# A four-layer kernel: the sequential stages of a batch rebuilt as a slotted pipeline over batches, scores through DRAM

## The chip, the core and the metric

The kernel runs on one core of a Trainium2 chip. The metric is the device time of one execution in microseconds, lower is better. A core has a matrix engine (TensorE; PE in the rows, PEld its weight loads), VectorE (DVE), ScalarE (ACT), GpSimd (POOL), and SyncE (SP), which here issues all DMA. Each engine runs its own queue of instructions strictly in order and meets the others only at semaphores.

## What is computed

The input is eight batches of 512 tokens with 128 features. Four residual layers follow one another, each closed by a layer norm without weights:

```
x = norm(x + attn0(x))    # 16 heads of 8, rotary, causal softmax
x = norm(x + ffn0(x))     # silu(x W1) * (x W2), then gelu(. H1), gelu(. H2), W3; hidden 512
x = norm(x + attn1(x))    # 16 heads of 64, 4 memory keys, l2-normed q and k:
                          #   dots = W_pre @ (10 q.k)   (heads mixed), causal
                          #   keep the 64 largest of each row, softmax, W_post @ attn
                          #   out = (attn @ v) * head_scale * sigmoid(x Wg + bg), then Wo
x = norm(x + moe(x))      # 16 experts of 64, top 4 of the softmaxed gates, and a shared expert
```

Batches don't depend on each other.

## The kernel before

**Stages.** `network` opens with `start` (first batch only), then a hardware loop over eight batches, whose body is `front`, a conditional `again`, and `experts`. Each is a block: five queues, one per engine, that all begin and end together, with the semaphores cleared behind it. `again` (a full selection of the 64 largest) runs only if a flag says that the quick search missed.

**`front`** does for batch b, in turn: attention 0 (transposed scores, L1182, exponentials on ACT at L1309 and L1312, products with values at L1196), the feed-forward layer (L1238, L1240, L1248, with Silu and Gelu at L1317 to L1321), keys and queries of attention 1 (L1269, L1272, squares and norms on DVE and POOL), then `scores_*`.

**`scores_*`** is the second attention. The 512 query rows are cut into 64 pieces of 8 rows (`R8`), each 8 rows x 16 heads = 128 partitions, and taken in pairs: 32 steps, with a pipeline behind each. A step's score rows are up to 516 wide (`width`), and the query tiles come in the order 3, 1, 0, 2 (`TILE_ORDER`). For one pair:
- PE makes q.k for two heads at a time (L614); ACT and, for the first tile, DVE scale and store it to `dots` in SBUF (L772, L989);
- SP loads eight rows of all heads from `dots` to `mixin`, SBUF to SBUF (L553);
- PE mixes heads (L666) and ACT copies the result to `xs` (L790);
- DVE takes the row maximum and moments (L857, L859), POOL a first threshold (L580 to L583), then three rounds: ACT counts what lies above it (L799), POOL corrects it (L589 to L591);
- ACT exponentiates (L810), DVE finds the exact 64th value near the threshold (L912 to L929) and masks (L952), POOL scales the post-mix weights by the row sum (L567, L574), PE mixes heads again, transposed (L679), ACT stores it (L821);
- once in four steps PE multiplies with the values (L705, L710), DVE gates (L963), and once in eight PE applies Wo (L719) and DVE adds the residual (L969).

The step loops of the engines (`for s in range(...)` in `scores_tensor`, `scores_scalar`, `scores_vector`, `scores_gpsimd`) write out by hand what of step s, s-1, s-2, s-3 and s-4 stands where. PSUM has four rings of two banks: a (PE to ACT), o (PE to DVE), m (head mix) and t (post mix). A matmul into a ring waits until the bank before last has been read.

**`experts`** does the fourth layer of batch b and beside it the rotary projections of batch b+1 (L1034 to L1046), their split into three bf16 parts on POOL (L1024 to L1028), their way through DRAM into the stacked layout (L1011, L1017), and the row maxima of attention 0 for the first eight heads (PE L1066 and L1070, DVE L1084). The other eight heads' maxima stand in `front`. The experts' products are L1463 (Silu on ACT, L1498), L1465 and L1468 (products on DVE, L1536 and L1540) and L1478.

## Time and profile before

| | us |
|---|---|
| median of 3 runs | 4687.48 |
| lowest and highest | 4676.58, 4687.7 |
| the profiled execution | 4677.0 |
| its span, first to last instruction | 4675.4 |
| busy: PE, DVE, ACT, POOL | 3245.3, 2600.1, 2074.2, 1379.7 |

The program is eight nearly identical batches. One of them, from 3531 to 4106 us of the span, is read here: `front` up to the first head mix (3531 to 3712), the second attention (3712 to 4015), `experts` (4015 to 4106). The steps of the second attention are timed by the DVE instruction L861, one for each pair.

### The profile page before, as it was taken

The numbers are of one execution on the slowest core, as the hardware profiler recorded it, in microseconds if no ns is written. First come the engines' busy times: TensorE is split into PE (matmuls) and PEld (weight loads), VectorE is DVE, ScalarE is ACT, GpSimd is POOL, SyncE is SP. The second block draws the span as 40 slices with busy tenths as digits, with TensorE's granted clock in tenths as the row PEclk, the third lists the DMA queues.
The fourth block names the chain that finished last, engine by engine and source line by source line (L and its number), as shares of the span: only waits on it lengthen the run. The fifth ranks groups of instructions, "written<-read, shape, count | busy, mean of one in ns | idle before, by whom it ended". The sixth has DMA issues, their size and how long they took to land. (4 is left out here: it accounts for less than half of the span.)

```text
span 4675.4 us, 63627 instructions
## 1 busy us (share of the span) xinstructions
PE 3245.3 (69%) x19124; PEld 1917.1 (41%) x19124; DVE 2600.1 (56%) x9042; ACT 2074.2 (44%) x5898; POOL 1379.7 (30%) x3919
## 2 busy tenths in 40 slices
PE   3777567675786757767667776687766777667766
PEld 1345423453334532345323453235532355323543
DVE  2367743666436664466643775437753477534774
ACT  1356413664226642266322763227622376124770
POOL 1035501354013540145301453014520145102551
PEclk6877778777687777977778777787787877778787
DMA  2021210212102120022200221002210112101111
GB/s 89 1 37 24 47 47 0 40 27 52 36 0 41 29 53 32 0 43 30 51 29 7 40 33 46 29 15 33 32 45 29 20 29 31 45 29 28 23 30 48
DMA packets 99769, 151.99 MB, mean 33 GB/s; under 512 B 19518, under 2 KB 86998, under 8 KB 96126
## 3 DMA queue, kind: packets, MB, share of 16 engines
q1 hardware_dynamic: 99326, 146.87, 15.4%
q8 instruction: 182, 2.98, 0.3%
q14 instruction: 261, 2.14, 0.1%
HBM read 64.90 MB, written 9.59 MB: 16 GB/s over the span
## 5 line engine op out<-in xcount | busy, mean ns | idle before, releaser
L666 PE MATMUL pm<-mixin,pre_b 128*128 128x258 f32 (+15 forms) x1088 | 466.7, 552 | 343.0 <-ACT xs L790 160.6
L505 POOL TENSOR_TENSOR rstd<-var,powers 128x4 f32<-128x4 f32 x32 | 32.5, 1015 | 1623.3 <-DVE var L515 1623.3
L679 PE MATMUL pt<-wsc,attn 128*128 128x128 f32 x2560 | 445.2, 333 | 87.0 <-POOL wsc L574 86.3
L614 PE MATMUL pa<-kT,qT 64*128 64x132 f32 (+3 forms) x1024 | 327.2, 533 | 239.8 <-ACT dots L772 128.7
L679 PEld LDWEIGHTS pt<-wsc,attn 128*128 128x128 f32 x2560 | 391.6, 236 | 168.5 <-POOL wsc L574 123.7
L799 ACT ACTIVATE ex<-xs,thr 128x420 f32<-128x420 f32 (+12 forms) x624 | 347.6, 560 | 179.2 <-POOL thr L591 149.6
L666 PEld LDWEIGHTS pm<-mixin,pre_b 128*128 128x128 f32 x1088 | 216.4, 244 | 478.4 <-issue 321.7
L1084 DVE TENSOR_REDUCE dots<-po 128x1 f32<-128x384 f32 (+3 forms) x374 | 222.9, 638 | 339.8 <-PE po L1070 339.8
L857 DVE MAX8 top<-xs 128x8 f32<-128x420 f32 (+15 forms) x384 | 163.5, 434 | 441.3 <-ACT xs L790 440.4
L589 POOL TENSOR_SCALAR shift<-signs 128x2 f32<-128x2 f32 x624 | 127.6, 205 | 677.7 <-ACT ex L799 340.7
L772 ACT ACTIVATE dots<-pa,rq 128x388 f32<-128x388 f32 (+3 forms) x512 | 228.0, 473 | 208.9 <-PE pa L614 169.9
L614 PEld LDWEIGHTS pa<-kT,qT 64*128 64x128 f32 x1024 | 168.2, 234 | 333.2 <-ACT dots L772 177.4
L705 PE MATMUL po<-at,vx 128*64 128x64 f32 x5120 | 241.0, 259 | 63.4 <-ACT at L821 59.4
L705 PEld LDWEIGHTS po<-at,vx 128*64 128x64 f32 x5120 | 222.2, 170 | 86.3 <-ACT at L821 71.2
L821 ACT COPY at<-pt 128x384 f32<-128x384 f32 (+3 forms) x512 | 196.1, 426 | 131.4 <-PE pt L679 130.8
L580 POOL TENSOR_TENSOR spreads<-meanvar,powers 128x2 f32<-128x2 f32 x208 | 157.1, 755 | 302.1 <-DVE meanvar L865 302.1
L574 POOL TENSOR_SCALAR wsc<-post_b,rsum 128x128 f32<-128x128 f32 x512 | 218.5, 437 | 26.2
L799 ACT ACTIVATE squares<-tokens,thr 128x452 f32<-128x452 f32 (+6 forms) x336 | 186.8, 559 | 88.0 <-POOL thr L591 64.8
L567 POOL TENSOR_TENSOR rsum<-ssum,powers 128x2 f32<-128x2 f32 x256 | 181.6, 709 | 113.7 <-DVE attn L952 96.4
L921 DVE MAX8 best<-left 128x8 f32<-128x420 f32 (+12 forms) x416 | 203.1, 488 | 0.0
L921 DVE MAX8 best<-squares 128x8 f32<-128x420 f32 (+12 forms) x416 | 198.9, 478 | 0.0
L799 ACT ACTIVATE squares<-xs,thr 128x420 f32<-128x420 f32 (+5 forms) x288 | 160.7, 562 | 74.2 <-POOL thr L591 60.8
(261 smaller groups left out, 7613.7 us busy)
## 6 DMA issues: line engine op xcount, KB each, us to landing
dots<-moe_dram SPq DMA_DIRECT2D x8, 2176.0 KB, 9.2
kT<-parts_dram SPq DMA_DIRECT2D x216, 64.0 KB
dots<-ffn_dram SPq DMA_DIRECT2D x8, 1536.0 KB, 6.8
at<-ffn_dram SPq DMA_DIRECT2D x8, 1280.0 KB, 10.7
mixin<-dots SPq DMA_DIRECT2D x32, 258.0 KB
mixin<-dots SPq DMA_DIRECT2D x32, 242.0 KB
mixin<-dots SPq DMA_DIRECT2D x32, 226.0 KB
parts_dram<-at SPq DMA_DIRECT2D x18, 384.0 KB, 4.0
```

Source lines behind the costliest of these rows:

```text
L567: chain.link(nc.gpsimd.tensor_tensor(rsum[:, p], ssum[:, p], powers[:, TT + PAIR:], ALU.pow))
L574: nc.gpsimd.tensor_scalar(wsc[:, m % A_SLOTS], post_b[:, :], rsum[:, p, z:z + 1], 1.0, ALU.mult, ALU.mult).then_inc(attn_done, 1)
L614: nc.tensor.matmul(bank_of(("qk", t, 2 * c + odd, z))[:, 0:jn], qT_v[at:at + HD1, c, P * t:P * t + P], kT_v[at:at + HD1, c, j0:j0 + jn], s ...
L666: ins = nc.tensor.matmul(bank[:, 0:jn], pre_b[:, :], mixin[:, m % MIX_SLOTS, j0:j0 + jn], start=True, stop=not last)
L679: ins = nc.tensor.matmul(bank[:, P * k:P * k + P], attn[:, m % A_SLOTS, P * k:P * k + P], wsc[:, m % A_SLOTS], start=True, stop=True)
L705: ins = nc.tensor.matmul(bank[at:at + HD1, col:col + RB], vx_v[:, k, HD1 * h:HD1 * h + HD1], at_v[:, k, h, :], start=k == 0, stop=k == t a ...
L772: nc.scalar.activation(dots[:, at:at + jn], banks_a[A.bank(key)][:, 0:jn], ACT.Copy, scale=rq[:, t, g:g + 1]).then_inc(a_free, 1)
L799: ins = nc.scalar.activation(ex[m % E1_SLOTS][:, 0:width(n)], xs[m % X_SLOTS][:, 0:width(n)], ACT.Sign, scale=-1.0, bias=thr[:, s % LIVE, ...
L821: nc.scalar.copy(at_v[:, 0:t + 1, :, R8 * u:R8 * u + R8], bank[:, 0:P * (t + 1)].rearrange("p (k h i) -> p k h i", k=t + 1, h=H1)).then_in ...
L857: found = chain.mark(nc.vector.max(out=top[:, p, z], in_=xs[m % X_SLOTS][:, 0:width(n)]))
L921: done[z] = chain.mark(nc.vector.max(out=best[:, z, 8 * k:8 * k + 8], in_=left[z][:, 0:wn]))
L1084: nc.vector.tensor_reduce(row_max[:, i, h:h + 2 * n - 1:2], scores, X, ALU.max).then_inc(o_free, 1)
```

## The change

The three stages of a batch become one block, `period`, in which the second attention of batch b is the backbone and everything else is hung beside it: the experts of batch b-1, and attention 0, the feed-forward layer, keys and queries and all q.k scores of batch b+1.

1. **Slots.** A step of the backbone gets four slots. `schedule()` is a table from slot to items; each engine's step loop calls `beside(4 * s + j)` at four fixed places, and each engine issues its own part of an item (`side_tensor`, `side_scalar`, `side_vector`, `side_gpsimd`, `side_sync`).
2. **Scores through DRAM.** All q.k scores of the next batch are made at the end of the period (items `qk`, all copied by ACT), stored in a ring of four SBUF slots (`fresh`), written by 32 DMAs to one of two DRAM buffers (item `dots`), and loaded back in the next period as contiguous rows.
3. **Rings.** The keys of rings a and o follow the new order (`Plan`). Attention 0's transposed scores use ring a for both heads of a pair, where they used a and m; its exponentials have one buffer of eight heads (`exps`), where there were two; the sums accumulate in ring o.
4. **Placement.** A new SBUF area `side` holds the side work's tiles; `xs`, `ex` and `left` get buffers of their own. `x2` and the transposed `xe` are copied by POOL at the start of a period.
5. **Frame.** `opening` makes batch 0's front alone, the loop runs eight periods, `closing` makes the last batch's experts alone. The first period runs experts on zeros, the last a front on a padded batch; both are thrown away. A batch has one block and one clearing of semaphores less.
6. Small: `cb` and the shared expert run on 128 partitions with zeros, `qs` gives 32 products of 16 columns where 8 of 512 stood, and attention 0's maxima of all sixteen heads follow each other.

```diff
+def schedule():
+    ...
+    one_by_one((-4, -4, -3, -3, -3, -2, -2, -1, -1, -1), [("split", z, i) for z in range(2) for i in range(5)])
+    one_by_one((-2, 0, 1, 3), [("parts", 0), ("parts", 1), ("stack", 0), ("stack", 1)])
+    one_by_one((0, 2, 4, 5, 7), [("x3T",), ("lg",), ("gexp",), ("gating",), ("cT",)])
+    for k in range(MC + 1):
+        put(8 + k, "m", k)
+        if k:
+            put(8 + k, "cb", k - 1)
+    for n in range(len(S_PAIRS)):
+        ...
+        put(12 + n, "s", n)
+    ...
+    products = (35, 39, 41, 43, 48, 51, 53, 55)
+    heads = ((31, 32, 33, 34), (35, 36, 37, 38), (39, 39, 40, 40), (41, 41, 42, 42),
+             (44, 45, 46, 47), (48, 49, 50, 50), (51, 51, 52, 52), (53, 53, 54, 54))
+    ...
+    one_by_one((66, 67, 68, 69), [("f", k) for k in range(KC)])
+    one_by_one((70, 71, 72, 73), [("h1", k) for k in range(KC)])
+    one_by_one((78, 79, 80, 81), [("h2", k) for k in range(KC)])
+    one_by_one((84, 85, 86, 88, 89, 90), [("y1", 0), ("y1", 1), ("norm", 3, "a"), ("norm", 3, "b"), ("x2T",), ("memk",)])
+    one_by_one((92, 93, 94, 95), [("k", t) for t in range(TT)])
+    one_by_one((96, 96, 97, 97, 98, 98, 99, 99), [("q", k) for k in range(NC)])
+    ...
+    for n in range(TT * NC):
+        put(109 + n // 2, "qk", n // NC, n % NC)
+        put(110 + n // 2, "dots", n // NC, n % NC)
...
+            out += mixes[:1] + self.beside(4 * s) + values + mixes[1:] + self.beside(4 * s + 1) + gates
+            out += posts[:1] + self.beside(4 * s + 2) + posts[1:] + self.beside(4 * s + 3)
...
+                sp.wait_ge(a_free, A.nth(("qk", o, k, len(pieces(wt)) - 1, 1)))
+                tile = dots_d[dots_at, ROWS_AT[t]:ROWS_AT[t + 1]].rearrange("(q n) -> q n", q=P)
+                sp.dma_start(tile[:, 2 * k * wt:2 * (k + 1) * wt], fresh[:, n % D_SLOTS, 0:2 * wt]).then_inc(dots_out[n % D_SLOTS], 16)
...
-                tile = dots[R8 * u:R8 * u + R8, SCORES_AT[t]:SCORES_AT[t] + H1 * wt].rearrange("p (g j) -> p g j", g=H1)
-                sp.dma_start(mixin[:, m % MIX_SLOTS, 0:wn], tile[:, :, 0:wn]).then_inc(mix_in[m % MIX_SLOTS], 16)
+                tile = dots_d[dots_in, ROWS_AT[t]:ROWS_AT[t + 1]].rearrange("(p j) -> p j", j=wt)
+                sp.dma_start(mixin[:, m % MIX_SLOTS, 0:wn], tile[P * u:P * u + P, 0:wn]).then_inc(mix_in[m % MIX_SLOTS], 16)
```

The first place is VectorE in the fourth layer. Before, in `experts`, the products (L1536) and then the row maxima of eight heads (L1084) follow each other with nothing between. Rows of before:

```order
L1536 TENSOR_TENSOR qT<-po,qT 128x512
L1536 TENSOR_TENSOR vx<-po,qT 64x512
L1084 TENSOR_REDUCE dots<-po 128x4 x2
L1084 TENSOR_REDUCE dots<-po 128x2 x4
L1084 TENSOR_REDUCE dots<-po 128x1 x16
```

In the changed kernel the same engine, over step 3 of the backbone (L1115 and L1120 are the experts' products, L1021 the row maxima; the others are the threshold search):

```order
L1453 TENSOR_SCALAR left,above<-xs,thr 128x420 x2
L1457 SCALAR_TENSOR_TENSOR left<-left,xs 128x420 x2
L1115 TENSOR_TENSOR side<-po,side 128x512
L1120 TENSOR_TENSOR side<-po,side 128x512
L1021 TENSOR_REDUCE side<-po 128x2 x2
L1463 MAX best<-left 128x8 x2
L1467 MATCH_REPLACE left<-best,left 128x420 x2
L1463 MAX best<-left 128x8 x2
L1471 SCALAR_TENSOR_TENSOR picked,bound<-cst,above,best 128x16 x2
L1115 TENSOR_TENSOR side<-po,side 128x512
L1120 TENSOR_TENSOR side<-po,side 128x512
L1021 TENSOR_REDUCE side<-po 128x2 x2
```

What moved: products and maxima now stand between the pieces of the search, four results from ring o at a time.

The second place is ScalarE. Before, the experts' Silu calls stand in one run after one table load:

```order
L1492 ACTIVATE gates_e<-dots 128x4x16
L1498 ACT_TABLE_LOAD
L1498 ACTIVATE qT<-pa 128x512 x8
L1498 ACTIVATE qT<-pa 64x512
```

In the changed kernel, in steps 2 and 3 (L975 is the Silu, L1334 the counting, L1345 the exponential):

```order
L975 ACT_TABLE_LOAD
L975 ACTIVATE side<-pa 128x512
L1317 COPY vx<-pa 128x512 x2
L975 ACTIVATE side<-pa 128x512
L1334 ACTIVATE ex,signs<-xs,thr 128x420 x2
L1345 ACT_TABLE_LOAD
L1345 ACTIVATE ex<-xs,negm 128x420 x2
L975 ACT_TABLE_LOAD
L975 ACTIVATE side<-pa 128x512
```

What moved: Silu and exponential alternate, with a table load at each change, 15 loads in a period.

The third place is ScalarE near the end of a period, steps 27 and 28: the next batch's scores (L963) stand between the counting rounds.

```order
L1356 COPY at<-pt 128x16x8 x2
L1362 COPY tail<-pa 4x2x16x8
L963 ACTIVATE side<-pa,rq 128x258 x8
L1334 ACTIVATE ex,signs<-xs,thr 128x324 x2
L1345 ACTIVATE ex<-xs,negm 128x292 x2
L963 ACTIVATE side<-pa,rq 128x258 x8
L1334 ACTIVATE ex,signs<-xs,thr 128x324 x2
L963 ACTIVATE side<-pa,rq 128x258 x8
```

What moved: before, these copies (L772) lay at the start of the second attention and ahead of each query tile, the odd heads of the first tile on DVE.

## Rows read from the trace of the kernel before

**Rows 1.** The page, parts 1 and 2: busy time, clock in 40 slices.

```profile
PE 3245.3 (69%) x19124; PEld 1917.1 (41%) x19124; DVE 2600.1 (56%) x9042; ACT 2074.2 (44%) x5898; POOL 1379.7 (30%) x3919
...
PEclk6877778777687777977778777787787877778787
```

**Rows 2.** Windows of one batch by stage: us, PE, PEld, DVE, ACT, POOL busy, clock, DMA.

```profile
3531.00:3712.00 181.00, 138.12 (x610) 61.14 (x610) 67.42 (x110) 56.28 (x118) 14.88 (x14) 0.81 0.05 16
3712.00:4015.00 303.00, 207.24 (x1566) 150.35 (x1566) 210.16 (x919) 195.30 (x607) 141.63 (x460) 0.76 0.20 33
4015.00:4106.00 91.00, 58.18 (x207) 28.17 (x208) 44.42 (x96) 8.39 (x13) 14.84 (x15) 0.76 0.24 63
```

**Rows 3.** Windows of second attention: steps to 1, 2-8, 9-13, 14-22, 23-26, 27-31.

```profile
3712.00:3734.20 22.20, 14.63 (x30) 5.96 (x31) 5.50 (x18) 10.00 (x26) 4.17 (x17) 0.73 0.43 76
3734.20:3813.20 79.00, 57.58 (x338) 38.21 (x337) 64.67 (x206) 62.97 (x163) 35.25 (x117) 0.76 0.20 34
3813.20:3857.20 44.00, 32.21 (x302) 27.29 (x302) 30.42 (x156) 29.97 (x112) 25.54 (x86) 0.77 0.17 25
3857.20:3912.10 54.90, 42.21 (x358) 32.02 (x357) 34.19 (x205) 33.17 (x117) 25.00 (x71) 0.81 0.12 19
3912.10:3939.30 27.20, 16.48 (x79) 10.36 (x80) 23.04 (x135) 18.82 (x75) 18.56 (x68) 0.69 0.40 62
3939.30:3980.40 41.10, 27.99 (x276) 22.92 (x275) 38.73 (x162) 32.33 (x101) 27.37 (x88) 0.81 0.15 22
```

**Rows 4.** Same windows, score work alone: ACT L772 (steps 9-13), PE L614 (14-22).

```profile
3813.20:3857.20 44.00, 3.85 (x12) 0.77 0.17 25
...
3857.20:3912.10 54.90, 10.71 (x32) 3.85 (x32) 0.81 0.12 19
```

**Rows 5.** Windows of `front`: attention 0; feed-forward; keys, queries and first scores.

```profile
3531.00:3606.00 75.00, 53.53 (x342) 20.90 (x342) 27.57 (x41) 25.44 (x67) 1.08 (x3) 0.67 0.09 35
3606.00:3660.00 54.00, 42.85 (x120) 20.67 (x120) 8.64 (x29) 11.40 (x15) 2.02 (x2) 0.92 0.00 0
3660.00:3712.00 52.00, 41.73 (x149) 19.57 (x148) 31.21 (x42) 19.44 (x36) 11.78 (x9) 0.89 0.04 6
```

**Rows 6.** DVE lines of one batch by form: count | busy us, mean ns | idle.

```profile
L1084 DVE TENSOR_REDUCE dots<-po 128x1 f32<-128x512 f32 x16 | 10.3, 687 | 9.4 <-PE po L1070 9.4
L1084 DVE TENSOR_REDUCE dots<-po 128x1 f32<-128x384 f32 x16 | 8.2, 553 | 6.4 <-PE po L1070 6.4
...
L1536 DVE TENSOR_TENSOR qT<-po,qT 128x512 f32<-128x512 f32 x8 | 5.5, 692 | 12.2 <-PE po L1465 12.2
```

**Rows 7.** The page, part 5: score copies on ACT, all batches.

```profile
L772 ACT ACTIVATE dots<-pa,rq 128x388 f32<-128x388 f32 (+3 forms) x512 | 228.0, 473 | 208.9 <-PE pa L614 169.9
```

**Rows 8.** Timeline of ACT at a table load: start us, us, engine, what.

```profile
3736.51 1.28 ACT L810 ACT_TABLE_LOAD   x1
3737.81 1.18 ACT L810 ACTIVATE ex<-xs,negm 128x420 f32<-128x420 f32 x2
```

**Rows 9.** Timeline of a layer norm on DVE beside a POOL memset.

```profile
4020.04 3.51 POOL L1439 MEMSET kT<- 128x4096 bf16 x1
4020.12 4.08 DVE L518 TENSOR_SCALAR og<-res,mv,rstd 128x128 f32<-128x128 f32 x4 [1.14 <-POOL rstd L505]
```

**Rows 10.** Timeline of one pair of row maxima, PE and DVE.

```profile
4076.07 0.12 PEld L1066 LDWEIGHTS po<-kT 48*128 48x128 bf16 x2 [0.81 <-DVE dots L1084]
...
4076.64 1.02 DVE L1084 TENSOR_REDUCE dots<-po 128x1 f32<-128x384 f32 x2 [0.68 <-PE po L1070]
```

**Rows 11.** Timeline of DVE from the last mask to `experts`.

```profile
3992.19 0.08 DVE L952 DVE_READ_ACCUMULATOR attn<-tokens,bound,squares 128x1 f32 x1
...
4007.38 0.14 DVE L1397 TENSOR_SCALAR flag<-flag_f 1x1 int32<-1x1 f32 x1
4013.71 0.49 DVE L510 BATCH_NORM_STATS2 stats<-res 128x6 f32<-128x128 f32 x2 [6.18 <-issue]
```

**Rows 12.** Window of `start`, the first batch's opening.

```profile
22.50:91.20 68.70, 17.68 (x66) 5.65 (x67) 20.78 (x34) 0.09 (x1) 8.76 (x12) 0.58 0.16 35
```

More of the change, by code:

```diff
@@ L1145, in _ @@
+                for z in range(D_SLOTS):
+                    sp.wait_ge(dots_out[z], 16 * TT * NC // D_SLOTS)
+                sp.wait_ge(x_in, 64)
             @block.gpsimd
@@ L1332, in _ @@
-                act.wait_ge(rq_done, 1)
-                scores_scalar(act, RINGS, False)
+                for slot in range(FIRST_SLOT, LAST_SLOT + 1):
+                    for what in OPENING.beside(slot):
+                        side_scalar(act, OPENING, what)
             @block.vector
@@ L1493, in _ @@
-                for k in range(MC + 1):
-                    n = P if k < MC else HID1
-                    bank = filled(("m1", k))
-                    if k >= 2:
-                        act.wait_ge(o_free, O.nth(("m3", k - 2)))
-                    nc.scalar.activation(silu1[0:n, k % 2], bank[0:n, :], ACT.Silu).then_inc(a_free, 1)
+                for slot in range(FIRST_SLOT, LAST_SLOT + 1):
+                    for what in CLOSING.beside(slot):
+                        side_scalar(act, CLOSING, what)
@@ L1541, in _ @@
-                for i, h in S_FIRST:
-                    row_maximum(filled, i, h)
-                split_maxima(dve, chain, O, filled, 0)
-                dve.wait_ge(a_full, A.nth("y3"))
-                chain.link(nc.vector.tensor_tensor(res[:, :, :], rows(banks_a[A.bank("y3")]), x3[:, :, :], ALU.add))
-                norm(dve, chain, 1, x4, x4_done)
+                for slot in range(FIRST_SLOT, LAST_SLOT + 1):
+                    for what in CLOSING.beside(slot):
+                        side_vector(dve, chain, CLOSING, what)
@@ L1548, in network @@
         with nc.Block() as block:
-            start(block)
+            opening(block)
         clear_semaphores()
@@ L1552, in network @@
             with nc.Block() as block:
-                front(block)
+                period(b, block)
             clear_semaphores()
@@ L1558, in network @@
                 with nc.Block() as block:
-                    again(block)
+                    again(b, block)
                 clear_semaphores()
-            with nc.Block() as block:
-                experts(b, block)
-            clear_semaphores()
+        with nc.Block() as block:
+            closing(block)
+        clear_semaphores()
 def constants():
```

1728 lines of the change are left out of this document (942 added, 786 removed).

## The prediction

> **What bounds the kernel now.** I read busy times first [rows 1]: no engine is near its span, and the busiest, PE, reaches 69%. So it is the order of the work that costs, and the stages have to be read apart. One batch takes 575 us [rows 2]: `front` 181, the second attention 303, the experts 91. In `front` and the experts PE works 138 and 58 us while ACT and POOL do little; these are chains in which one engine at a time is late. In the second attention DVE (210), PE (207) and ACT (195) are all about two thirds busy. The sum over the three stages is PE 403.5, DVE 322, ACT 260, POOL 171 us per batch. This is what the change can work with: with everything side by side a batch could not go under DVE's 322 us, nor under what PE needs.
>
> PE's need depends on its clock. The granted clock of the batch is 0.76 to 0.81 of full speed by stage [rows 2] and goes to 0.92 where PE is busy 43 of 54 us [rows 5]; the levels are 1.2 and 2.4 GHz. 403.5 us at 0.78 are some 315 us at full clock. DVE and PE would then be near each other.
>
> **What the side work adds to each stretch of the backbone.** The new block is the old second attention, whose 32 steps I group by what the slot table hangs beside them. For each group I take the busy time of the engine that comes out longest: its backbone part from [rows 3], less the q.k scores that leave (they move to the end, [rows 4]), plus the side part.
>
> - Steps -1 to 1: the backbone's own filling took 22 us. New beside it are a norm, the rotary products and, on POOL, the memset of 3.5 us [rows 9] and ten operations of the split. SP can't issue the second half's load before the split is through, and loads of the backbone queue behind it. I take 28.
> - Steps 2 to 8 (experts, all row maxima): DVE 64.7 of backbone. Side: the experts stage has 44.4 us of DVE [rows 2], of which some 8 (norm, rotary) fall before step 2; to it come the other eight heads' maxima, half of 44 reductions at 0.55 to 0.69 us [rows 6], 14 us, and their split, 3. So 53, together **118**. PE has 57.6 of backbone, part of it scores that leave, and less beside than DVE: it stays under.
> - Steps 9 to 13 (attention 0): ACT 30.0 less 3.9 [rows 4] plus three quarters of its 25.4 us [rows 5] is 45. PE, with 32.2 less the scores, comes out as long, and they take turns: **48**.
> - Steps 14 to 22 (feed-forward beside the narrow tile): PE 42.2 less 10.7 [rows 4], plus 42.9 [rows 5] and 5 for sums: **79**. Here the backbone is short and the side work sets the pace.
> - Steps 23 to 26 (keys, queries): DVE 23.0 plus 31.2 [rows 5] less the 16 score copies and the first maxima that are in it, some 9: **45**. PE is equal.
> - Steps 27 to 31 (all scores): ACT 32.3 plus 80 copies (64 as before, 16 from DVE) at 0.473 us [rows 7], 37.8: **70**.
> - Steps 32 and 33: 12. The drain, from the last mask to the flag, was 15.2 us [rows 11] and stays, since nothing is hung beside it. Block end, flag and the first DRAM load: the old boundary had 6.2 us before DVE moved [rows 11]; I take 7.
>
> The floor is 28 + 118 + 48 + 79 + 45 + 70 + 12 + 15 + 7 = **422 us** per period.
>
> **What it loses above the floor.** Before, the groups took 79.0, 44.0, 54.9, 27.2 and 41.1 us where their busiest engine had 64.7, 32.2, 42.2, 23.0 and 38.7 [rows 3]: factors of 1.22, 1.37, 1.30, 1.18 and 1.06, 1.22 over all. The factor falls as the busiest engine fills: where DVE has 94% of the stretch it is 1.06. The first of them also holds waits for SBUF copies of a new query tile, which the prefetch from DRAM takes away. But new waits come: each side item ties queues together. The row maxima show the price: DVE idles 0.68 us ahead of a pair and PE waits 0.81 us for the bank [rows 10], in 22 pairs 15 us, and DVE idled 12.2 us ahead of eight experts' products [rows 6]. DVE now has search work to put between, so I count part of it. I take a factor of 1.12 on the five groups (360 us): 43 us. Ends: 1.06, the best stretch, 22 us; 1.22, the old mean, 79 us. The period is **465 us** (444 to 501), against 575.
>
> **Costs that I set to nothing, and their cover.** Table loads go from 7 to 15 in a batch. The row shows 1.28 us and the next ACTIVATE 1.30 us after the load's start [rows 8], so 8 x 1.3 = 10 us of ACT. They stand in steps 2 to 5, 16 to 18 and 25, where DVE or PE is the longest by 5 us and more a step. If that cover is gone they cost 8 x 10 = 80 us in the whole program. The Trainium skill (ScalarE: Activation LUTs, What ACT_TABLE_LOAD costs) has about 2.66 us for a switch, with a drain, and its rule is to batch calls by table set, which speaks against alternating Silu and exponential; by that price it would be 21 us a period and, uncovered, 170 us in all. The trace doesn't agree with the drain: the load begins as the last read of the accumulator ends.
>
> POOL's long operations can hold DVE: the norm's four operations took 4.08 us beside a memset of 3.51 us [rows 9], about 3 us too long. The split, the squares of q and two copies now run beside DVE's search, at most 25 us a period if each blocked DVE for its whole length, nothing if none overlapped. I leave it inside the factor. The Trainium skill (SBUF — State Buffer, the part on port contention) tells of one port pair that VectorE and GpSimd lock in turn; for these rows the trace agrees.
>
> The DMA share was 0.20 in the second attention and 0.05 in `front` [rows 2]. The scores add 10.6 MB written (16 heads x 512 rows, 132 to 516 wide) in five steps. ACT waits for a slot of the ring of four only if a write takes longer than the copies of three items. Nothing to something: I take nothing, and make it a rival.
>
> **Opening and closing.** The program's head and `start` end at 91 us [rows 12]. `front` to the first mix is 181 more [rows 2], 272. Added: the second set's maxima alone, 19; attention 0 with one exponential buffer, 12; the rest of the scores on ACT, 22. The loop begins at **325**. Closing is the experts stage of 91 us less 20 for the maxima: **71**.
>
> **Sum.** 325 + 8 x 465 + 71 = 4116 us, against the profiled execution's own 4677.0 (span 4675.4). The median of the runs is 10 us higher than that execution; I give **4120**.
>
> **Rivals.**
> *Tight fit.* The side work fills the holes as filled stretches do now, factor under 1.06: under 444 us a period, under 3950; worked out at 1.03, 433 us, it is 3860. For it: the last group of rows 3 ran within 6% of DVE's pace. Against: rings of two banks. Chance 0.12.
> *The old looseness stays.* Factor 1.22 (1.17 to 1.30): waits for the threshold rounds between ACT and POOL are not filled but joined by the ring waits. 501 us a period, 4404. For it: the mean of rows 3. Chance 0.25.
> *Scores through DRAM become the wait.* In steps 27 to 31 ACT waits for landings. If an item takes 3 us instead of the 1.2 of its copies, 32 x 1.8 = 58 us a period: 523, so 4580. Against: low DMA share. Chance 0.05.
> *Lockstep, slower than before.* Four in-order queues meet at four slots a step; an engine that waits in a slot for a result holds the backbone work queued behind it, and this holds the others: PE behind ring o, DVE behind Silu, ACT behind the counts. The change breaks even at (4677 - 396) / 8 = 535 us, a factor of 1.31 on the groups, 2.3 us a step more than forecast. At 1.4 it is 566 us and 4924. For it: steps 9 to 13 had 1.37 without side work. Against: those were loose because no engine was full. Chance 0.07.
>
> **How the numbers follow.** Forecast case, factors 1.06 to 1.17, 3950 to 4270: 0.49. Tight 0.12, loose 0.25, DRAM 0.05, lockstep 0.07; something else within 0.3% of before 0.02. (0.3% is what a measurement here can tell from no change.) Faster: 0.12 + 0.49 + 0.25 + 0.05 = 0.91, of which I move 0.02 to slower for what I haven't seen; same 0.02, slower 0.09. The range leaves out the lockstep, the DRAM case, the upper part of the loose one and the lower half of the tight one: 3880 to 4480.
>
> **What the profile after would show.** Eight periods of some 465 us; DVE over 65% busy and PE over 70%, with a clock above 0.80; DVE nearly full in steps 2 to 8, ACT in 27 to 31, PE in 14 to 22; no wait of PE for `mixin`. Wrong if DVE is well under 85% in steps 2 to 8 (ring o or Silu is late), if ACT waits on a DMA at the scores, or if the opening is far from 325 us.

## Result: slower, 4846 us against 4687

The changed kernel took 4845.6 us (median of 4 runs, 4838.5 to 4852.0) against 4687.4 of the kernel before: 1.034 times its time (95% interval 1.032 to 1.036). The forecast was 4120 us, range 3880 to 4480. It was wrong in its sign and by 726 us. All times compared here are of undisturbed (fast) executions, so one of the two of tanh_experts is left aside.

The page of the changed kernel, part 1 and the clock's line of part 2; they answer to [rows 1]. PE went from 69% to 72% of the span, and the clock line moves between 0.5 and 0.8, where it moved between 0.6 and 0.9 before:

```profile
span 4845.8 us, 68143 instructions
PE 3480.1 (72%) x20366; PEld 2193.9 (45%) x20366; DVE 2597.4 (54%) x8879; ACT 2292.2 (47%) x6292; POOL 1397.7 (29%) x3960
PEclk6758786787868786787867786777867877687867
```

From part 5, the two rows on the scores, which answer to [rows 7] (L854 makes the products, L963 copies them to SBUF):

```profile
L854 PE MATMUL pa<-side 64*128 64x258 f32 (+3 forms) x1440 | 475.2, 624 | 121.5 <-ACT side L963 121.2
L963 ACT ACTIVATE side<-pa,rq 128x258 f32<-128x258 f32 (+3 forms) x720 | 307.1, 474 | 333.0 <-PE pa L854 317.7
```

PE waits for ACT and ACT waits for PE: each is the other's releaser.

One period of the changed kernel (the flag is the last result of a period). The lines are: boundary; start and step -1; steps 0 and 1; 2 to 8; 9 to 13; 14 to 22; 23 to 26; 27 to 30; 31 to the flag. The first two lines are those behind this period's flag, where the next one starts. Columns as in [rows 2].

```profile
3678.10:3686.60 8.50, 0.00 (x0) 0.00 (x0) 0.00 (x0) 0.00 (x0) 0.02 (x1) 0.65 0.12 17
3686.60:3706.00 19.40, 11.97 (x36) 5.42 (x36) 12.30 (x25) 4.82 (x8) 13.32 (x13) 0.80 0.51 170
3149.90:3172.90 23.00, 8.55 (x17) 3.16 (x16) 7.42 (x36) 8.88 (x23) 7.92 (x24) 0.61 0.71 126
3172.90:3319.10 146.20, 103.31 (x596) 63.84 (x596) 109.75 (x292) 70.83 (x165) 35.94 (x118) 0.82 0.12 34
3319.10:3391.70 72.60, 56.13 (x490) 35.92 (x491) 35.64 (x156) 46.09 (x159) 26.14 (x87) 0.71 0.11 30
3391.70:3486.30 94.60, 75.46 (x464) 50.48 (x464) 48.36 (x232) 40.69 (x117) 24.32 (x72) 0.90 0.10 27
3486.30:3548.20 61.90, 47.95 (x201) 33.26 (x200) 45.03 (x155) 31.09 (x99) 32.74 (x80) 0.67 0.08 21
3548.20:3639.60 91.40, 77.68 (x329) 47.14 (x328) 31.63 (x124) 56.37 (x155) 20.12 (x67) 0.65 0.31 117
3639.60:3678.10 38.50, 24.56 (x302) 20.58 (x302) 21.79 (x78) 16.41 (x43) 10.98 (x34) 0.73 0.06 23
```

The forecast took step 31 together with 27 to 30:

```profile
3548.20:3660.00 111.80, 88.88 (x459) 56.70 (x459) 48.72 (x183) 70.15 (x190) 29.45 (x97) 0.66 0.28 103
```

In these windows PE is the longest engine from step 9 on. The forecast had ACT there in steps 27 to 31; ACT's 70.2 us came out as forecast, but PE has 88.9. And where PE is fullest, in steps 27 to 30 (77.7 of 91.4 us), its mean granted clock is 0.65, lower than in any other stretch of the steps from 2 on.

The loop begins at 369 us, eight periods take 553 us each (546 the first, the others 553 to 556), and from the last flag to the end it is 62 us, of which the boundary is 9. Before, the loop began at 91 us and eight batches took 573 us each. So a period gains 20 us, 160 in all, but the pipeline has 331 us more outside its periods: 369 + 8 x 553 + 53 = 4846, before 91 + 8 x 573 = 4675.

### The profile page after: what moved, and what is told of

Its sections match the earlier page's. It is cut to its first block and busy times, and to the rows that moved or that the text cites. A ratio compares the mean times of both kernels' runs of the same rounds, so it can differ in the third digit from the quotient of the medians.

```text
span 4845.8 us, 68143 instructions
## 1 busy us (share of the span) xinstructions
PE 3480.1 (72%) x20366; PEld 2193.9 (45%) x20366; DVE 2597.4 (54%) x8879; ACT 2292.2 (47%) x6292; POOL 1397.7 (29%) x3960
## 5 line engine op out<-in xcount | busy, mean ns | idle before, releaser
L1334 ACT ACTIVATE ex<-xs,thr 128x420 f32<-128x420 f32 (+12 forms) x1248 | 694.8, 563 | 309.0 <-POOL thr L1187 136.6
L854 PE MATMUL pa<-side 64*128 64x258 f32 (+3 forms) x1440 | 475.2, 624 | 121.5 <-ACT side L963 121.2
L963 ACT ACTIVATE side<-pa,rq 128x258 f32<-128x258 f32 (+3 forms) x720 | 307.1, 474 | 333.0 <-PE pa L854 317.7
L1496 DVE SCALAR_TENSOR_TENSOR attn<-xs,bound,ex 128x420 f32<-128x420 f32 (+14 forms) x480 | 238.9, 528 | 296.7 <-issue 218.4
L854 PEld LDWEIGHTS pa<-side 64*128 64x128 f32 x1440 | 238.9, 265 | 319.8 <-ACT side L963 245.0
L927 ACT ACTIVATE side<-pa 128x256 f32<-128x256 f32 (+3 forms) x576 | 220.0, 434 | 305.0 <-PE pa L759 256.4
L1021 DVE TENSOR_REDUCE side<-po 128x1 f32<-128x384 f32 (+3 forms) x396 | 234.7, 633 | 97.0 <-PE po L734 95.7
L713 PE MATMUL pa<-side 128*128 128x512 f32 x576 | 261.7, 599 | 6.0 <-DVE side L1049 5.2
L1356 ACT COPY at<-pt 128x384 f32<-128x384 f32 (+3 forms) x512 | 194.2, 434 | 135.3 <-PE pt L1252 68.8
L1334 ACT ACTIVATION_READ_ACCUMULATOR ex<-xs,thr 128x1 f32 x1248 | 243.8, 195 | 0.0
L1345 ACT ACTIVATE ex<-xs,negm 128x228 f32<-128x228 f32 (+15 forms) x512 | 238.8, 515 | 2.3 <-POOL thr L1187 1.6
```

Source lines behind the costliest of these rows:

```text
L713: ins = nc.tensor.matmul(bank[:, :], wgt[:, HID0 * j + P * k:HID0 * j + P * k + P], src[:, j, :], start=j == 0, stop=j == KC - 1)
L854: nc.tensor.matmul(a_bank(what + (z, odd))[:, 0:jn], qT_v[at:at + HD1, k, P * t:P * t + P], kT_v[at:at + HD1, k, j0:j0 + jn], start=True, ...
L927: nc.scalar.activation(exps[:, 2 * a + odd, 0:S - P * k], filled(what + (odd,))[:, 0:S - P * k], ACT.Exp, scale=SCALE0).then_inc(a_free, 1)
L963: nc.scalar.activation(fresh[:, n % D_SLOTS, wt * odd + j0:wt * odd + j0 + jn], filled(what + (z, odd))[:, 0:jn], ACT.Copy, scale=rq[:, t, ...
L1021: nc.vector.tensor_reduce(row_max[:, i, h:h + 2 * n - 1:2], scores, X, ALU.max).then_inc(o_free, 1)
L1334: ins = nc.scalar.activation(ex[:, m % E1_SLOTS, 0:width(n)], xs[:, m % X_SLOTS, 0:width(n)], ACT.Sign, scale=-1.0, bias=thr[:, s % LIVE, ...
```

## Experiments

Times are compared with sp_late (4686.5 us), unless said otherwise; that kernel came out level with the kernel before (ratio 1.000, 0.999 to 1.002). Every kernel but bare, no_front and no_experts has its edit. The kernel before, timed beside each group of runs, took 4683 to 4694 us, so differences under some 15 us between runs of different groups are not read. "A period" is the mean from flag to flag in the trace.

### What each part costs: three kernels that leave work out

Edits: the plan of a period; where front is left out, the loads come from the first score buffer, and SP's waits for what is left out go too (not shown). `bare` has neither flag, `no_front` (shown) only experts, `no_experts` only front.

```diff
-        PERIOD = Plan(True, experts=True, front=True)
+        PERIOD = Plan(True, experts=True, front=False)
-                scores_sync(sp, PERIOD, b & 1, beside)
+                scores_sync(sp, PERIOD, 0, beside)
```

> Leaves out of the eight periods the next batch's work (front) and the last batch's experts; the scores of batch 0 are loaded from DRAM in every period, the last batch's experts still run in closing. Outputs of the other batches are not the network's. What is left is opening, eight second attentions fed from DRAM, closing. Theory A (the side work is what the period pays for, the DRAM path and the new boundary are nearly free): the old second attention took 303 us, of which some 35 us were score copies and filling, so 265 to 285 us a period, with opening 380 and closing 80 together 2580 to 2740 us. Rival B (loads from DRAM and the new boundary themselves cost 30 us a period or more): 300 to 315 us a period, 2860 to 2980 us.

> Leaves out the next batch's attention, feed-forward and keys from the periods; experts beside the second attention stay. Theory A (each side adds its own price, and the prices add up to the 553 us of a period): the experts cost 50 to 70 us over the bare period, so about 335 us a period and 3140 us in all. Rival C (lockstep: the sides are cheap alone and dear together): 15 to 30 us over bare, about 300 us a period, 2860 us in all; then the sum of the two prices over the bare period stays 40 us or more under 553.

> Leaves out the experts from the periods; the next batch's attention, feed-forward and keys stay. Theory A: front costs 200 to 220 us over the bare period (PE alone needs 138 us for it at its clock), so 480 to 500 us a period and about 4350 us in all; steps 9 to 31 take what they took with experts, and only steps 2 to 8 get shorter. Rival C: 150 to 170 us over bare, 430 us a period, 3900 us in all.

Measured: bare 2634 us, 277 a period; no_front 2847 us, 303 a period; no_experts 4490 us, 510 a period. So the experts cost 26 us beside the bare backbone and 43 on top of front; front costs 233. The two prices over bare add up to 536, and the period is 553: only 17 us come from having both. Rival B falls (bare is at 277). Rival C had no_front nearly right (2860 us), but falls by its own condition, which wanted 40 us or more. Theory A holds in the sum but not in its parts: experts were cheaper, front 13 to 33 us dearer than expected. Without experts steps 2 to 8 fell by 28 us, as theory A had it; but steps 27 to 30 fell too, from 91.4 to 85.4 us, which it had not, and the start by 6. What is dear sits in front.

How dear shows beside the kernel before. There the experts took 91 us and front 181 [rows 2]; the scores inside the second attention cost at most 26 more (its 303 us less bare's 277), so that front and scores were some 207, an estimate. Here the experts cost 43 and front 233. So the experts gained 48 us a batch by standing beside the backbone, and front lost some 26 against running alone. No run separates front from the backbone that it stands beside; that part of the lockstep isn't tested by the small interaction of 17 us.

### The start of a period: SP stands behind POOL's split (sp_late)

```diff
-    one_by_one((-2, 0, 1, 3), [("parts", 0), ("parts", 1), ("stack", 0), ("stack", 1)])
+    one_by_one((2, 3, 5, 7), [("parts", 0), ("parts", 1), ("stack", 0), ("stack", 1)])
```

> The two writes of the split parts and the 24 reads into the stacks move in SP's order from slots -2, 0, 1, 3 to 2, 3, 5, 7, behind the loads of the mixes. Nothing else changes. Theory A (PE waits for mixin at the start of a period because SP stands waiting for POOL's split with the loads queued behind it; 163 us in all in the trace, 20 a period): 12 to 20 us a period less, 4690 to 4750 us. Rival D (steps 1 and 2 are late anyway through Silu and ring o): within 30 us of 4846.

Measured: 4686.5 us, 159 less than the changed kernel; a period of 532 us, 21 less. Waits around the start of one period (us in all, times, longest), the changed kernel:

```profile
PE pm L1241 <- DMA mixin<-dots_scratch: 21.0, 3, 9.9
SPq L606 <- POOL side L666: 16.9, 2, 13.4
```

and sp_late:

```profile
PE pm L1241 <- DMA mixin<-dots_scratch: 2.0, 2, 1.2
SPq L606 <- POOL side L666: 9.2, 2, 5.2
```

SP still waits for POOL, but no load of `mixin` that PE is about to need stands behind it, and PE's wait went from 21.0 to 2.0 us. Of the 21 us a period, 11 lie between the flag and step 2, 5 in steps 2 to 8 and most of the rest behind step 27. Theory A holds; the gain is 1 us above its upper end.

### The scores in steps 27 to 30: which engine, or which ring

no_qk leaves the products, copies and writes of the scores out of the periods; every period loads from the first score buffer (not shown).

```diff
         def mine(what):
+            if what[0] in ("qk", "dots") and self.experts:
+                return False
```

> On the kernel sp_late (4686.5 us, 532 us a period). Leaves out of the periods the 80 products of queries and keys, their copies by ACT and the writes to DRAM; every period loads the scores of batch 0. Theory A (PE is what steps 27 to 31 wait for: 52.8 us of busy time a period at a granted clock near 0.62): these steps fall back to the bare pace of 7 to 9 us each, 55 to 65 us a period less, 4170 to 4250 us. Rival (ACT's 80 copies, 34 us a period, set the pace, as the forecast had it): 34 to 40 us less a period, 4370 to 4410 us. The granted clock of these steps without the products tells whether it is the products that keep it low.

Measured: 4231 us, 476 a period, 57 less, in theory A's range. Steps 27 to 30 fell from 88.9 us to these 33.1, and the clock rose to 0.80:

```profile
3140.50:3173.60 33.10, 21.58 (x173) 17.20 (x172) 31.22 (x124) 25.47 (x79) 19.16 (x65) 0.80 0.10 25
```

That spoke for PE as the bound; but both engines go with the products, so it could not tell PE's own work from its hand-over to ACT. The next three kernels could.

two_rings puts the items with odd k on the other PSUM ring, with DVE as reader; two_rings_act does the same with ACT as the only reader (it waits for `o_free` of the item ahead, and so does DVE at `av` and `wo`, to keep the ring's order).

```diff
-        return [what + (z, odd) for z in range(len(pieces(MEM + P * (t + 1)))) for odd in range(2)], []
+        keys = [what + (z, odd) for z in range(len(pieces(MEM + P * (t + 1)))) for odd in range(2)]
+        return ([], keys) if rest[1] % 2 else (keys, [])
...
+            elif name == "qk" and rest[1] % 2:
...
+                        nc.vector.tensor_scalar(fresh[:, n % D_SLOTS, wt * odd + j0:wt * odd + j0 + jn], filled(what + (z, odd))[:, 0:jn],
+                                                rq[:, t, h:h + 1], None, ALU.mult).then_inc(o_free, 1)
```

> On sp_late. Of the 32 items of scores the 16 with odd k go through ring o and are scaled by DVE (which is 35% busy there); the 16 with even k stay on ring a and ACT. PE's work is the same. Theory G (the pairs of products alternate with ACT's two copies: one pair every 1.8 us, of which PE's products are 1.2 us; it is the ring that costs): steps 27 to 30 go from 89 us to about 70, 15 to 20 us a period less, 4520 to 4570 us. Rival A (PE's own time at its low clock is the bound, it is 83% busy): at most 5 us a period, 4640 to 4680 us.

> As two_rings (4405 us, against 4686.5 of sp_late): the items of scores with odd k go through ring o. But ACT makes all the copies, as in sp_late, and DVE none. Theory G (what costs on one ring is that PE and its reader take turns; then PE has holes, its granted clock is 0.67 and its products take longer): most of the 281 us is kept, 4400 to 4480 us, and the clock in steps 27 to 30 stays above 0.85. Rival (it was the load taken from ACT): ACT has 34 us of copies again, 4620 to 4690 us.

qk_twice leaves the ring alone and gives PE twice the products:

```diff
+                        for last in range(2):
+                            ins = nc.tensor.matmul(bank[:, 0:jn], qT_v[at:at + HD1, k, P * t:P * t + P],
+                                                   kT_v[at:at + HD1, k, j0:j0 + jn], start=True, stop=True)
+                        ins.then_inc(a_full, 1)
```

> On sp_late, one ring. Each product of queries and keys is issued twice into its bank before ACT is told; PE has twice the columns there. Theory H (the clock follows how full PE is kept: with its holes filled by the second product it rises to 0.9 and above, so that the doubled work takes about the time of the single): steps 27 to 30 at 85 to 100 us against 89, 4680 to 4800 us. Rival (clock given by something else, 0.67 as before; PE's busy time doubles): 45 to 55 us a period more, 5050 to 5130 us.

Measured: two_rings 4405 us, 281 less; two_rings_act 4573, 114 less; qk_twice 4715, 28 more. Steps 27 to 30 in each, first sp_late:

```profile
3431.90:3520.80 88.90, 73.88 (x330) 46.06 (x328) 31.70 (x123) 55.86 (x154) 19.74 (x67) 0.69 0.32 120
```

qk_twice:

```profile
3447.80:3535.70 87.90, 73.06 (x486) 49.99 (x484) 31.50 (x123) 55.65 (x154) 20.72 (x67) 0.98 0.32 121
```

two_rings_act, then two_rings:

```profile
3351.80:3430.00 78.20, 64.21 (x335) 41.95 (x333) 31.76 (x123) 58.02 (x154) 19.72 (x67) 0.79 0.36 136
```

```profile
3238.80:3296.50 57.70, 50.88 (x339) 33.87 (x338) 47.14 (x162) 41.07 (x119) 18.93 (x69) 0.98 0.49 181
```

The number to see is the one behind POOL's busy time, the granted clock. With 80 products more (156 of their 160 records are in the trace), qk_twice takes as long as sp_late and PE is busy as long, because the clock is 0.98 in place of 0.69. The same 258 columns take 575 ns a record in sp_late and 403 in qk_twice. First sp_late, then qk_twice, by form, same windows:

```profile
L854 PE MATMUL pa<-side 64*128 64x258 f32 x64 | 19.7, 575 | 4.8 <-ACT side L963 4.8
```

```profile
L856 PE MATMUL pa<-side 64*128 64x258 f32 x128 | 22.2, 403 | 5.1 <-ACT side L966 5.1
```

So "PE is 83% busy" was no bound set by the amount of its work: with twice the products of the scores it was busy as long. Its time was long because the granted clock was low, and the clock rose when PE had more to do between ACT's copies. One item of the changed kernel, PE and ACT apart, shows the turns (start, duration, idle time before it):

```profile
3556.42 1.23 PE L854 MATMUL pa<-side 64*128 64x258 f32 x4
3558.21 1.59 PE L854 MATMUL pa<-side 64*128 64x258 f32 x4 [0.56 <-ACT side L963]
```

```profile
3557.68 0.84 ACT L963 ACTIVATE side<-pa,rq 128x258 f32<-128x258 f32 x2 [0.31 <-PE pa L854]
3559.47 0.84 ACT L963 ACTIVATE side<-pa,rq 128x258 f32<-128x258 f32 x2 [0.95 <-PE pa L854]
```

A pair of heads every 1.79 us, of which ACT needs 0.84. Theory G holds for two_rings, whose gain (31 us a period, and 36 in the opening) was above its range: in steps 27 to 30 PE's busy time fell by 23 us, with the clock, and its idle time by 8. For two_rings_act neither side was right: 4573 lies between 4480 and 4620, and its clock, 0.79, is under the 0.85 that theory G wanted. The second ring alone is worth 114 us (28 of them in the opening, 10 a period); the other 167 need DVE as the second reader, which takes ACT from 55.9 us of 88.9 to 41.1 of 57.7. DVE as a second reader on the one ring was not tried. Theory H holds for qk_twice and rival A falls.

### The squares of q in step 25 (qs_512, root_later)

qs_512 takes the products as the kernel before did, with `pick` as weights, then transposes:

```diff
-                    for k in range(NC):
-                        at = H1 - 2 - 2 * k
-                        ins = nc.tensor.matmul(bank[:, H1 * t:H1 * t + H1], squares_of(k)[:, P * t:P * t + P], c("pick")[:, at:at + H1],
-                                               start=k == 0, stop=k == NC - 1)
+                for k in range(NC):
+                    at = H1 - 2 - 2 * k
+                    ins = nc.tensor.matmul(bank[0:H1, :], c("pick")[:, at:at + H1], squares_of(k), start=k == 0, stop=k == NC - 1)
...
+            elif name == "qsT":
...
+                    ins = nc.tensor.transpose(bank[:, H1 * t:H1 * t + H1], q_norm[:, P * t:P * t + P], ident[0:H1, 0:H1])
```

> On sp_late. The sums of the squares of q go back to 8 products of 512 columns with `pick` as weights, a square root over 16x512, and 4 transposes, in place of 32 products with 128x128 weights and 16 columns (14 us in one piece on PE). Theory: step 25 goes from 27.4 us to about 18, 8 to 10 us a period less, 4605 to 4625 us. Rival (at the low clock the 512 columns take PE as long, and two more hand-overs come to it): within 15 us of 4686.

Measured: 4667.5 us, 19 less. Step 25 went from 27.4 to 23.7 us, the whole period by less than 2, and the opening by 5. That is nearer to the rival. root_later adds a slot between the products and the root (keys and scores follow a slot later):

```diff
-    one_by_one((102, 103, 103, 103, 103, 104, 104), [("qs",), ("qsT",), ("knorm",)] + [("kmul", t) for t in range(TT)])
+    one_by_one((102, 103, 104, 104, 104, 104, 105, 105), [("qs",), ("qroot",), ("qsT",), ("knorm",)] + [("kmul", t) for t in range(TT)])
```

> As qs_512 (4667.5 us), but ACT takes the square root one slot after PE's products, behind its last count of the step, and knorm, keys and scores start a slot later. In qs_512 ACT stood 8.8 us and DVE 10.2 us in step 25 while PE worked, since ACT waited for the products with its counts queued behind. Theory (in-order queues: the wait in the wrong place costs, not the products): step 25 falls from 23.7 to about 16 us, 5 to 9 us a period less, 4595 to 4625 us. Rival (the step is PE's anyway): within 15 us of 4667.

Measured: 4705 us, 38 more than qs_512. The local effect is there: step 25 fell to 19.6 us. The waits around step 25, the changed kernel:

```profile
ACT rq L950 <- PE pa L836: 14.0, 1, 14.0
DVE rq L1073 <- ACT rq L950: 13.4, 1, 13.4
PE pa L836 <- POOL side L682: 5.8, 1, 5.8
```

qs_512:

```profile
DVE rq L1080 <- ACT rq L957: 9.7, 1, 9.7
ACT side L955 <- PE pa L836: 8.8, 1, 8.8
```

and root_later:

```profile
ACT side L955 <- PE pa L836: 5.1, 1, 5.1
DVE top L1405 <- ACT xs L1332: 9.4, 1, 9.4
```

But step 26 grew by 2.8 us. Step 27 fell by 4.8 and step 28 grew by 4.6, which only moved work; and what was set a slot later, the scores, ended later: from step 31 to the flag it took 42.6 us against 37.4. Both were wrong: the wait in the middle was real, and removing it by a delay of everything behind it cost more.

### Banks asked for in pairs (by_bank)

The diff shows attention 0's transposed scores; its row maxima, on ring o, were changed the same way.

```diff
-                banks = [a_bank(what + (odd,)) for odd in range(2)]
                 for odd in range(2):
-                    at = RB * odd
-                    nc.tensor.matmul(banks[odd][:, 0:S - P * k], k_stack[at:at + STACK, h, P * k:P * k + P],
+                    bank, at = a_bank(what + (odd,)), RB * odd
+                    nc.tensor.matmul(bank[:, 0:S - P * k], k_stack[at:at + STACK, h, P * k:P * k + P],
                                      q_stack[at:at + STACK, h, P * k:S], start=True, stop=False)
-                for odd in range(2):
-                    nc.tensor.matmul(banks[odd][:, 0:P], identb, mask_t, start=False, stop=True).then_inc(a_full, 1)
+                    nc.tensor.matmul(bank[:, 0:P], identb, mask_t, start=False, stop=True).then_inc(a_full, 1)
```

> On sp_late. The row maxima's scores and the transposed scores of attention 0 take one bank, write and close it, and only then ask for the second; before, both banks had to be empty before the first product, so that PE and its reader took turns. Theory E (the looseness above the busiest engine is made by rings of two banks that are asked for in pairs; PE waited 156 and 130 us in all for them): 10 to 20 us a period less, 4530 to 4610 us, with steps 9 to 13 shorter by 2 to 3 us each. Rival F (PE's own time sets the pace there): under 3 us a period, 4665 to 4690 us.

Measured: 4623 us, 63 less: 6 us a period (steps 9 to 13 from 72.6 to 69.4) and 14 in the opening. That is between E and F: asking for the banks one at a time gives back only a part of PE's waits for them.

### Attention 0 in steps 9 to 13 (no_mask, best_st_twice)

no_mask drops the mask's product and closes the group with the scores; best_st_twice, on the kernel best (below), issues the scores twice.

```diff
-                                     q_stack[at:at + STACK, h, P * k:S], start=True, stop=False)
-                for odd in range(2):
-                    nc.tensor.matmul(banks[odd][:, 0:P], identb, mask_t, start=False, stop=True).then_inc(a_full, 1)
+                                     q_stack[at:at + STACK, h, P * k:S], start=True, stop=True).then_inc(a_full, 1)
```

```diff
+                    for last in range(2):
+                        nc.tensor.matmul(bank[:, 0:S - P * k], k_stack[at:at + STACK, h, P * k:P * k + P],
+                                         q_stack[at:at + STACK, h, P * k:S], start=True, stop=not last)
```

> On sp_late. Leaves out the triangular mask of the transposed scores of attention 0: 64 products of 128 columns a period, 9.1 us of PE's busy time per 52 records in steps 9 to 13. The values are not the network's. Theory A (PE at a granted clock of 0.69 paces steps 7 to 13): 6 to 10 us a period less, 4600 to 4640 us. Rival (ACT's exponentials and the hand-over pace them): under 3 us a period, above 4660 us.

Measured: 4639 us, 48 less, in theory A's range by the total and under it by the period: 3.8 us of it are in steps 9 to 13 (68.8 for 72.6), and 5 us in the opening. PE's work there does set the time, though not one for one with the 9 us that left.

> On best (4102.5 us, 489 us a period). The transposed scores' products of attention 0 (64 a period, in steps 7 to 13) are issued twice into their bank. Theory H carried over (the clock follows how full PE is kept): it rises from 0.75 to 0.9 in steps 9 to 13 and the time stays, 4080 to 4140 us. Rival (PE is not short of work there, 0.91 busy; the clock stays and the doubled products add their 10 to 18 us a period): 4180 to 4250 us.

Measured: 4165 us, 62 more than best. Steps 9 to 13, best and then best_st_twice:

```profile
2936.30:3005.90 69.60, 62.93 (x497) 37.45 (x498) 35.37 (x155) 46.70 (x157) 25.62 (x86) 0.76 0.09 25
```

```profile
2989.70:3060.40 70.70, 65.56 (x551) 35.88 (x550) 35.58 (x156) 47.82 (x158) 25.07 (x84) 0.86 0.09 25
```

Here the clock rose too, 0.76 to 0.86, and the doubled products cost these steps 1.1 us. On the mean of the periods, steps 7 to 13, which hold the doubled products, grew by 4.7 us, the opening by 12, and steps 27 to 30 by 2.0, for which no cause was shown. The total lies between theory and rival. As a remedy it loses; as a sign it says that in steps 9 to 13 as well a good part of PE's busy time was its clock.

### Scores over more slots (spread)

```diff
-        put(109 + n // 2, "qk", n // NC, n % NC)
+        put(105 + n * 5 // 8, "qk", n // NC, n % NC)
```

with the feed-forward, keys and queries 1 to 4 slots earlier.

> On sp_late. The feed-forward's items move up by 1 to 3 slots, keys and queries by 4, and the 32 items of scores are spread over 20 slots (105 to 124) in place of 16. No work changes. Theory A (PE is the bound there at its clock, work only moves): within 5 us a period, 4650 to 4720 us. Rival (the alternation of PE and ACT in a crowded stretch costs, and the gaps of the feed-forward are idle): 10 to 20 us a period less, 4530 to 4610 us.

Measured: 4652 us, 34 less, at the edge of theory A. Steps 27 to 30 fell by 19 us, 14 to 22 rose by 10 and 23 to 26 by 7: time mostly moved with the work.

### Table loads (tanh_experts)

```diff
-                nc.scalar.activation(silu1[:, k % 2], bank[:, :], ACT.Silu).then_inc(a_free, 1)
+                nc.scalar.activation(silu1[:, k % 2], bank[:, :], ACT.Tanh).then_inc(a_free, 1)
```

> On sp_late (4686.5 us). The experts' Silu becomes Tanh, which lies in the table of the exponentials, so that 6 of the 15 table loads of a period go, 7.7 us of ACT in steps 2 to 4; the experts' values are not the network's. Forecast's view (covered by DVE or PE): within 20 us of 4686, 4666 to 4706. Rival (they stand on the path, at 1.3 us each or more): 8 to 16 us a period, 4560 to 4620 us. The Trainium skill (ScalarE: Activation LUTs, What ACT_TABLE_LOAD costs) has about 2.66 us for a switch, the upper end.

Measured, in one execution: 4715 us, 9 us over the upper end of the forecast's view and far from the rival's 4560 to 4620. The trace counts 9 loads a period where sp_late has 15. Six loads fewer bring nothing that shows, so they look covered, as the forecast had it; one execution can't show more than that.

### The last period without front (peeled), and all together (best, best_spread)

```diff
+        LAST = Plan(True, experts=True)
...
-        with nc.Fori(0, B) as b:
+        with nc.Fori(0, B - 1) as b:
+            one_batch(b, PERIOD)
+        one_batch(B - 1, LAST)
```

> On sp_late. The last of the eight periods, whose front works on a batch that does not exist (zeros behind the input), is written out without front. Theory (pipeline's fixed cost: the last period takes the 303 us of no_front and not the 532 of the others): 225 to 235 us less in all, 4445 to 4470 us. Rival (more program, colder code: the written-out period is slower by tens of us): 4480 to 4520 us.

Measured: 4448 us, 238 less, as the theory had it: the written-out period took 294 us. The last period's front had worked on zeros.

> sp_late, two_rings, by_bank, qs_512 and peeled together. If the gains add up (281, 63, 19 and 238 us under 4686.5): 4085 us. If by_bank and two_rings repair the same holes: up to 4150. If keeping PE fuller raises its clock in the neighbouring steps too: down to 4030.

> best, with the feed-forward, keys and queries some slots earlier and the scores over 20 slots, as in spread (34 us under sp_late there). Theory: with the second ring the crowding at the end no longer costs, so within 20 us of best. Rival: the same 30 us less.

Measured: best 4102.5 us, **0.873 of the kernel before** (0.871 to 0.875); the four gains over sp_late add up to 601 us, and 584 are there, so the losses are nearly separate. That the result is near the forecast's 4120 us is chance: the 238 us of peeled and the edits of two_rings and by_bank are no part of the forecast. best_spread 4173, 71 more: with the second ring, moving work forward only crowds steps 14 to 22 (101.1 us against 93.2) and 23 to 26 (62.1 against 58.3). It is worse than both expectations. The page of best, part 1:

```profile
span 4100.4 us, 64651 instructions
PE 3130.2 (76%) x19198; PEld 1892.9 (46%) x19198; DVE 2643.1 (64%) x9072; ACT 2081.5 (51%) x5793; POOL 1377.0 (34%) x3936
```

## Why the prediction was wrong, step by step

| part of a period | forecast | measured | what it was |
|---|---|---|---|
| boundary | 7 | 8.5 | right |
| start, steps -1 to 1 | 28 | 42.4 | SP behind the split (sp_late: 11 us here, 5 in steps 2 to 8) |
| steps 2 to 8 | 118 x 1.12 = 132 | 146.2 | DVE 110 busy, 8 under the sum; the factor was 1.33 |
| steps 9 to 13 | 48 x 1.12 = 54 | 72.6 | PE 56 us at clock 0.71; ACT 46, as forecast |
| steps 14 to 22 | 79 x 1.12 = 88 | 94.6 | near |
| steps 23 to 26 | 45 x 1.12 = 50 | 61.9 | one item of 14 us on PE, the others wait for it |
| steps 27 to 31 | 70 x 1.12 = 78 | 111.8 | one ring; PE 89 at clock 0.66, not ACT 70 |
| steps 32, 33, drain | 27 | 18.1 | shorter |
| sum | 465 | 556 | |

**The step that failed** is the factor of 1.12 on the five groups, and with it the engine that was costed in steps 27 to 31. The busiest engines of the five windows have 109.8 + 56.1 + 75.5 + 48.0 + 88.9 = 378 us, against the forecast's 360; the windows took 487. So the factor was 487 / 378 = 1.29 on what was measured, and 1.35 on the forecast's own sum. Of 84 us missed in these groups, 487 - 1.12 x 378 = 64 are the factor and 1.12 x 18 = 20 the sum.

The argument for 1.12 was circular. A factor of time over the busiest engine's time is one divided by that engine's busy share; "the factor falls as the busiest engine fills" says the same thing twice. 1.12 claimed that the busiest engine would be busy 89% of each stretch. It was 82% before [rows 3], and 78% now. The group that had shown 1.06 was DVE on its own backbone; front's items hand over from engine to engine, and the old `front` was the row to take their factor from: 181 us with PE busy 138 [rows 2], 1.31.

What stood in the place of that looseness is measured for the larger part. Of the 88 us by which a period is over 465, the start is 21 (sp_late), the one ring and one reader of the scores 31 (two_rings), the banks in pairs 6 (by_bank). With these and qs_512, `best` has 491 us a period; the last 26 us over the forecast have no experiment that names them.

**The rival that came nearest** is the lockstep, with its chance of 0.07. Its break-even was a factor of 1.31, 535 us; measured are 1.35 and 553, between that and its case of 1.4 (566 us, 4924). "The old looseness stays" (1.22, 501 us) is further off. The mechanism was in part the lockstep's: loads stood behind SP's wait for POOL, ACT's counts behind its wait of 14.0 us for the squares, PE and ACT took turns on one ring. These are two queues at a time and not four; and of experts and front together only 17 us come on top of their single prices.

**PE's total** was on the table and not used. The forecast put 403.5 us of PE's work into 465 us, 87% busy, where no stage of before had more than 76% [rows 2]; it excused this by a clock that would rise ("403.5 us at 0.78 are some 315 at full clock"). The mean clock over the run came to 0.75, under the 0.78 of before.

**Steps 27 to 31, the wrong engine.** The term counted ACT's busy time, 32.3 + 37.8 = 70, and ACT did need 70.2. PE was not added up there. From the same rows it comes out longer: 28.0 of backbone [rows 3] and five times the 10.7 us that 16 of the 80 products took in steps 14 to 22 [rows 4], 81.5 us, an estimate; measured are 88.9. PE alternated with ACT on two banks, at a low clock. A row of before already had ACT waiting 169.9 us for these products [rows 7]; the prediction took its mean duration and passed over the wait.

**The start.** The prediction said that loads of the backbone queue behind SP's wait, and then took 28 us and forecast no wait of PE for `mixin`. The mechanism was seen and not priced: 21 us a period in all.

**Opening and closing.** The loop began at 369 us, not 325; with two_rings it begins at 333, so 36 of these 44 us are the scores on one ring. From the last flag it was 62 us, less the boundary 53, against 71. The ninth front, on zeros, was in the sum as the eighth full period; peeled shows it at 238 us. This was no error of the sum, but a cost of the change that could be taken out.

**Costs set to nothing.** Table loads: 15 a period as counted (before it was 6, not 7), and they look covered, by one execution. DRAM: ACT waited for no landing at the scores, the writes took 1.7 to 2.7 us; the DRAM rival falls. bare (277 us a period with all its loads from DRAM, against 303 for the old stage, which also made the scores) gives no sign that the loads are dear. POOL against DVE's port was not tried apart; in sum DVE was busy 312 us a period against 322 for a batch before, so its work did not get longer.

**Its own signs of being wrong.** Two of three came: DVE was busy 75% of steps 2 to 8, and the opening is 44 us from 325. ACT waited for no DMA at the scores.

## What to carry to other kernels

Before a schedule is costed by its busiest engine, divide each engine's total by the period that comes out: a share above any that the kernel has shown needs a reason. A "factor over the busiest engine" is the reciprocal of such a share and no evidence for it. Price each side of the work apart before hanging it beside another: the experts gained by it, front, whose items go from engine to engine, did not. Where a producer and a reader share a ring of two, look at the ring first; a second ring with a second reader was worth 281 us here, eight times what moving the same work to other slots brought (34). And what an in-order DMA queue waits for must come behind what others wait for, which was worth 159 us for four numbers.

## What the runs showed of the hardware that was not expected

PE's clock answered to how its products were issued. In steps 27 to 30 the same products ran at a mean granted clock of 0.69 in turns with ACT, at 0.98 when each was issued twice, at 0.79 with a second ring and ACT as the only reader, and at 0.98 with a second ring and DVE as second reader. The two levels are 1.2 and 2.4 GHz, so PE was at the lower one for more than half of the stretch in the first case and hardly in the others. Without any scores (no_qk) it was 0.80. So PE's busy share says little by itself: all of PE's work of that stretch was 73.9 us at 0.69 and 50.9 us at 0.98.

Nor does the busy share give the clock. two_rings had 0.98 with PE busy 88% of steps 27 to 30; by_bank in steps 9 to 13 had 0.75 with PE busy 90%:

```profile
3156.00:3225.40 69.40, 62.40 (x476) 36.50 (x476) 36.28 (x159) 44.96 (x150) 24.99 (x82) 0.75 0.08 19
```

What exactly brings the clock down was not tried apart.
